# A four-layer graph network on one core: edge rows joined to sender rows in source order, and layer 1 computed beside its gather

## The chip, the cores and the metric

The kernel runs on 1 core of one Trainium2 chip. The metric is the device time of one execution in microseconds, median of three runs. Five engines work side by side, each with its own queue of instructions: PE (matmul), DVE (vector), ACT (scalar), POOL (GpSimd) and SP (which here only issues DMAs). They wait for one another and for DMAs by semaphores.

## The reference

3125 nodes with 64 features, 53125 directed edges `src -> dst` sorted by `dst`. Four layers, each `x = x + layer(relu(layernorm(x)))`:

```python
# layer 0: per source node, over its edges
feat = concat(seg_sum(edge_attr_32, src), seg_max(edge_attr_32, src), seg_mean(edge_attr_32, src), u)
out0 = relu(feat @ W1 + b1) @ W2 + b2
# layer 1: attention, 8 heads; loops are added to the edges
hx = h @ W; a_src, a_dst = per-head dot products of hx
logits = leaky_relu(a_src[src] + a_dst[dst], 0.2)
alpha = softmax of logits over the edges of each dst
out1 = mean over heads of segment_sum(hx[src] * alpha, dst) + bias
# layer 2: message = silu(concat(edge_attr_64, h[src], h[dst]) @ W1_msg + b1_msg)
out2 = upd(h, segment_mean(message @ W2_msg + b2_msg, dst))      # upd: two dense layers with silu
# layer 3: cosine similarity of Wh[src] and Wh[dst], weighted, summed over the edges of each src
```

`message @ W1_msg` splits into three parts: an edge part (`edge_attr_64` by the first 64 rows of `W1_msg`), a sender part and a receiver part.

## The kernel before, in words

The edges and one extra entry for each node, M = 56250, form a list of L = 128 x 440 entries. Two such orders exist: by source (`K.by_src`) and by destination (`K.by_dst`). Entry (p, j) is the place p*440 + j, so each of the 128 partitions holds 440 entries in a row. Sums over a node's edges are scans along the partition (`tensor_tensor_scan` with a mask that is 0 where a node begins), and a carry across partitions (`collect`). Work goes in NBLK = 10 blocks of TB = 44 columns. A column is fetched by one indirect DMA that POOL issues: 128 rows of a DRAM table, chosen by 128 indices. `gather_blocks` issues the 440 columns of a layer into a ring of two blocks (RING = 2); POOL waits until the block two before has been used.

The order of the work:

- `sort_sources`: a bitonic network on DVE (137 steps, 512 columns; short distances across partitions go through PE transposes and an ACT copy, `turn_blocks`, `keep_partners`) orders the list by source. In the same step `EdgeTable` multiplies `edge_attr_64`, given transposed as `edges_t`, by `W1_msg` on PE, ACT copies the result (line 610) and stores it as the table `recp`: an edge's row is the edge part and its source node (RE = 66 words).
- `layer0_pass`: POOL issues 440 gathers of `rec_s` rows (line 878; R0 = 36 words: `edge_attr_32`, two weights, the other node) in source order. DVE meanwhile sorts again (`sort_destinations`, here with two words for each entry, 1024 columns), `edge_order`, `list_setup` and `src_to_tiles` make index lists and masks, and `layer0_sums` scans block by block: ACT fills masks and turns rows (`fill`), DVE scans sums and maxima, ACT packs (`pack`), SP stores `sums0`.
- `layer0_finish`: POOL issues 22 edge gathers (`early_edges`, line 1351), 25 gathers of `sums0` at the last entry of each node (`collect`, line 1008), 60 more edge gathers; DVE and PE form the carries (line 1057 is the first use of the gathered sums), then two dense networks give the nodes and layer 1's table `tab1`.
- Layer 1: `layer1_gather` (line 831, 440 columns of R1 = 82 words) is stored as `g1` in tile order. When all of it is in, `layer1_softmax` works on 110 partitions x 512 entries (lines 1572 to 1625), `layer1_spread` makes the item weights, and `layer1_sums` runs 54 bodies of 12 items: DVE makes the weights (line 1847), PE multiplies (line 1831), DVE adds into `acc` (line 1855). Window, place and slot of each item are read into registers (line 1874). `layer1_tail` (from line 2029) divides by the sums, finishes x and stores the sender and receiver parts as table `tab2` of 2 x 3200 rows of R2 = 128 words. Beside all this POOL issues the remaining 358 edge gathers (lines 1379 and 1370) and eight stores of finished blocks to `rowsd` (line 1332).
- Layer 2: `layer2_gather` waits for `tab2` and the edge rows. POOL gathers 440 columns of `tab2` rows by the source node that came along in the edge row, word 64 of `u`. Each block: ACT turns the receiver half (line 2358), DVE scans it over the node's entries (line 2399), adds the edge part `u` (line 2407) and the sender half (line 2411), ACT applies silu, DVE scans, SP stores `sums2`. `layer2_tail` collects and makes layer 3's table.
- Layer 3: the same way in source order.

An engine's steps follow one another (`Step`); with `pool_ahead=True` POOL isn't held at the end of a step, so that its gathers run ahead of the other engines. `renew_semaphores` resets semaphores that counted far.

## Time and profile before

| | |
|---|---|
| runs | 3940.43, 3941.34, 3942.44 us, median 3941.34 |
| span of the profiled execution | 3095.7 us |
| the profiled execution's own time | not given; against the median of the runs 845.6 us lie outside the span |
| POOL busy | 2190.4 us (71%), 2299 instructions |
| DVE busy | 1326.6 us (43%) |
| PE busy | 610.1 us (20%) |
| ACT busy | 481.9 us (16%) |
| HBM | 154.17 MB read, 93.09 MB written, 80 GB/s over the span |

Busy time leaves out the issuing of DMAs on other engines, registers and semaphores. The span runs from the first to the last instruction of the program that the profiler recorded. Times in the timeline are counted from the span's start.

### The profile page before, as it was taken

How to read it: one execution, taken by the hardware profiler on the slowest of the kernel's cores; microseconds unless marked ns; L12 is line 12 of the kernel's file. 1: busy time of each engine (PE TensorE's matmuls, PEld its weight loads, DVE VectorE, ACT ScalarE, POOL GpSimd, SP SyncE). 2: the span in 40 equal slices, each digit the busy share in tenths (PEclk: the TensorE clock that was granted, in tenths of full speed). 3: DMA queues.
4: the chain of work that ended last, by engine and by line, in shares of the span. 5: the costliest groups of instructions: out<-in, count | busy, mean ns of one | idle time of the engine just before them, and what ended most of it. 6: DMA issues, size and time to landing. Idle time of an engine off the chain costs nothing.

```text
span 3095.7 us, 14532 instructions
## 1 busy us (share of the span) xinstructions
PE 610.1 (20%) x3300; PEld 466.1 (15%) x3301; DVE 1326.6 (43%) x1981; ACT 481.9 (16%) x447; POOL 2190.4 (71%) x2299
## 2 busy tenths in 40 slices
PE   5521130001410000001888860000000400000001
PEld 5411110001300000001676640000000300000001
DVE  8888885202310000008466643233244615353455
ACT  2200006211100000000000022223223212111220
POOL 0177777777777777777777777777777377777774
PEclk8665565555555555555899875555555555555555
DMA  9311114212344755645355424323232123223231
GB/s 325 112 25 14 14 27 100 64 34 63 66 52 53 67 57 60 65 52 65 106 135 155 111 50 74 109 91 128 91 109 92 45 56 85 78 72 91 72 90 52
DMA packets 192274, 248.04 MB, mean 80 GB/s; under 512 B 135507, under 2 KB 146381, under 8 KB 184662
## 3 DMA queue, kind: packets, MB, share of 16 engines
q0 software_dynamic: 74048, 114.24, 19.1%
q1 hardware_dynamic: 60102, 103.67, 10.0%
q10 hardware_dynamic: 58064, 29.51, 7.9%
q14 instruction: 45, 0.37, 0.0%
q8 instruction: 15, 0.25, 0.0%
HBM read 154.17 MB, written 93.09 MB: 80 GB/s over the span
## 4 chain that ended last, share of the span: by engine, by line
POOL 55%; issue 19%; DVE 2%; ACT 0%; DMA 0%; DVEq 0%; POOLq 0%; ACTq 0%
POOL l1g_rows L831 13%; POOL l2g_rows L831 13%; POOL l3g_rows L831 12%; POOL ep_rows L1370 11%; POOL ep_rows L1351 2%; POOL l2t_res L2457 1%; POOL l3t_res L2866 1%; POOL l0f_res L1008 1%; DVE l3g_banks L2813 0%; DVE l3g_banks L2837 0%; ACT l3g_banks L2771 0%; DVE l3g_banks L2834 0%; DVE l3g_dot L2820 0%; DVEq L2819 0%; POOL ep_rows L1379 0%
## 5 line engine op out<-in xcount | busy, mean ns | idle before, releaser
L878 POOL DMA_INDIRECT l0g_rows<-in_rec_s,ents x440 | 427.4, 971 | 137.6 <-issue 133.9
L831 POOL DMA_INDIRECT l2g_rows<-tab,ep_rows x440 | 416.8, 947 | 134.2 <-issue 134.2
L831 POOL DMA_INDIRECT l1g_rows<-tab,srct x440 | 416.8, 947 | 134.2 <-issue 134.2
L831 POOL DMA_INDIRECT l3g_rows<-tab,others x440 | 416.1, 946 | 134.2 <-issue 134.2
L1370 POOL DMA_INDIRECT ep_rows<-recp,entd x352 | 338.7, 962 | 107.3 <-issue 107.3
L1572 DVE TENSOR_TENSOR l1s_A<-l1s_bank,l1s_mk 110x512 f32<-110x512 f32 x8 | 5.2, 686 | 528.4 <-PE l1s_bank L1534 528.4
L1831 PE MATMUL l1a_pa<-l1a_g,l1a_wt 128*128 x1296 | 169.6, 291 | 0.0
L1831 PEld LDWEIGHTS l1a_pa<-l1a_g,l1a_wt 128*128 128x128 f32 x1296 | 158.9, 202 | 23.8 <-issue 23.8
L2811 DVE COPY l3g_banks<-l3g_q 128x65 f32<-128x65 f32 x12 | 2.7, 229 | 306.8 <-ACT l3g_banks L2771 306.4
L2397 DVE COPY l2g_mix<-l2g_q 128x64 f32<-128x64 f32 x11 | 2.5, 228 | 306.9 <-ACT l2g_mix L2358 306.9
L1534 PE MATMUL l1s_bank<-ident,atp 128*110 128x128 f32 x64 | 10.9, 347 | 539.7 <-ACT atp L1473 530.6
L2872 PE MATMUL l3t_nmp<-ident,l3t_nmb 128*64 128x128 f32 x2 | 0.7, 447 | 575.0 <-DVEq L2889 575.0
L1847 DVE TENSOR_TENSOR l1a_wt<-l1a_place,item_ex 128x1536 f32<-128x1536 f32 x54 | 94.9, 1757 | 7.7
L1351 POOL DMA_INDIRECT ep_rows<-recp,entd x82 | 79.1, 964 | 25.0 <-issue 24.7
L319 POOL IOTA iot<- 128x3200 f32 x1 | 2.8, 2803 | 130.0 <-DVE sorts_raw L335 130.0
L1473 ACT COPY atp<-l1g_rows 128x704 f32 (+1 forms) x10 | 8.3, 826 | 552.5 <-DMA l1g_rows<-tab,srct 552.5
L1534 PEld LDWEIGHTS l1s_bank<-ident,atp 128*110 128x110 f32 x64 | 10.4, 217 | 540.4 <-issue 531.1
L2771 ACT COPY l3g_banks<-l3g_rows 128x2860 f32<-128x2860 f32 (+3 forms) x12 | 55.2, 4599 | 220.8 <-DMA l3g_rows<-tab,others 220.7
L420 DVE TENSOR_TENSOR sortd_x<-sortd_x 128x512 f32<-128x512 f32 (+1 forms) x128 | 85.6, 669 | 4.2
L2872 PEld LDWEIGHTS l3t_nmp<-ident,l3t_nmb 128*64 128x64 f32 x2 | 0.3, 203 | 575.2 <-DVEq L2889 575.2
L421 DVE TENSOR_TENSOR sortd_x<-sortd_x 128x512 f32<-128x512 f32 (+1 forms) x128 | 84.5, 660 | 0.0
L2358 ACT COPY l2g_mix<-l2g_rows 128x2816 f32<-128x2816 f32 (+2 forms) x11 | 47.5, 4318 | 231.6 <-DMA l2g_rows<-tab,ep_rows 231.6
(582 smaller groups left out, 2330.2 us busy)
## 6 DMA issues: line engine op xcount, KB each, us to landing
l1a_g<-g SPq DMA_DIRECT2D x54, 390.0 KB
recp<-ep_rows ACTq DMA_DIRECT2D x11, 1320.0 KB, 5.9
g<-l1g_rows ACTq DMA_DIRECT2D x10, 1430.0 KB, 22.7
sums<-l0s_sums SPq DMA_DIRECT2D x10, 1408.0 KB, 5.1
sums<-l2o_sums SPq DMA_DIRECT2D x9, 1408.0 KB, 4.9
sums<-l3o_sums SPq DMA_DIRECT2D x9, 1408.0 KB, 5.3
rowsd<-ep_rows POOLq DMA_DIRECT2D x8, 1452.0 KB, 5.9
ep_rows<-rowsd SPq DMA_DIRECT2D x8, 1452.0 KB, 6.6
```

Source lines behind the costliest of these rows:

```text
L420: v.tensor_tensor(out[0], pair[0], pair[1], ALU.min).then_inc(step, 1)
L421: v.tensor_tensor(out[1], pair[0], pair[1], ALU.max).then_inc(step, 1)
L831: nc.gpsimd.indirect_dma_start(out=ring.rows[:, s, j, :], out_offset=None, in_=table, in_offset=bass.IndirectOffsetOnAxis(ap=index(b, s, j ...
L878: nc.gpsimd.indirect_dma_start(out=rows[:, j, :], out_offset=None, in_=K.a["rec_s"], in_offset=bass.IndirectOffsetOnAxis(ap=K.by_src.ent[: ...
L1008: nc.gpsimd.indirect_dma_start(out=res[:, w, :], out_offset=None, in_=table, in_offset=bass.IndirectOffsetOnAxis(ap=end[:, w:w + 1], axis= ...
L1351: nc.gpsimd.indirect_dma_start(out=ring.rows[:, s, j, :], out_offset=None, in_=K.recp, in_offset=bass.IndirectOffsetOnAxis(ap=K.by_dst.ent ...
L1370: nc.gpsimd.indirect_dma_start(out=ring.rows[:, s, j, :], out_offset=None, in_=K.recp, in_offset=bass.IndirectOffsetOnAxis(ap=K.by_dst.ent ...
L1831: nc.tensor.matmul(pa[b][:, bass.ds(places[u], P)], wt[:, b, u].rearrange("p h s -> p (h s)"), g[:, b, bass.ds(slots[u], P)], start=False, ...
L1847: v.tensor_tensor(wt[:, b], place[:, b].unsqueeze(2).to_broadcast([P, IB, H, WIN]), K.item_ex[:, :, bass.ds(n * IB, IB)].rearrange("p h i ...
L2358: nc.scalar.copy(cut(bank_of(i), n)[:, :, 1:], ring.rows[:, b % RING, c0:c0 + n, D:].rearrange("p j f -> p f j")).then_inc(spread, 1)
L2457: nc.gpsimd.indirect_dma_start(out=res[:, w, :], out_offset=None, in_=K.sums2, in_offset=bass.IndirectOffsetOnAxis(ap=by.end[:, w:w + 1], ...
L2771: nc.scalar.copy(cut(bank_of(i), C1, n)[:, :, 1:], ring.rows[:, b % RING, c0:c0 + n, C1:].rearrange("p j f -> p f j")).then_inc(spread, 1)
```

## The change

- `rec_s` rows grow to RR = 100 words, with `edge_attr_64` at their end; `edges_t`, `others`, `EdgeTable`, `recp` and `rowsd` go. Layer 0's gather fills a ring of two blocks, and POOL saves blocks 0 to 7 to `recd`; the sums load them back.
- `layer0_sums` also makes the edge part of layer 2 for blocks 0 to 8 (`EdgeRows`: ACT `move`, PE `project`, DVE `differ`), and a new `last_edges` that of block 9. It stores, in source order, the difference of each entry's edge part to the entry before it in the same run of one source, into `tabT`.
- `sort_destinations` sorts one word for each entry; `edge_order`, `early_edges` and `remaining_edges` go.
- Layer 1: `layer1_softmax`, `layer1_spread` and `layer1_sums` go. `layer1_items` and a new `layer1_marks` (masks of the nodes that cross a block's border) come ahead of a new `layer1_stream`, which does the softmax of each block as it lands, then 3 or 4 bodies (the last block 21), then 16 steps of a third sort (`OrderSort`), which gives for each entry in destination order its place in source order. Nodes that cross a border are joined in `layer1_borders`.
- `layer1_tail` writes the sender part, by 25 indirect DMAs, to the first entry of each source (`begin`) in `tabT`, and sender and receiver part to its end. A new step `source_rows` loads `tabT` block by block, scans it along each source's run and stores it back, so that each row becomes sender part plus edge part.
- `layer2_gather` gathers rows of 64 words of `tabT` by place (`by_dst.ent`); the receiver part is the row of a node's own entry, picked out by a DVE multiply in place of the ACT turn.

```diff
-R0 = 36
-RE = 66
+RR = 100
+SAVED = NBLK - 2
+QB = 11
+QH = H * QB
+SORT_STEPS = 137
+SORT_SHARE = 16
...
-            layer0_finish(K)
...
-                    layer1_gather(K)
-                    layer1_softmax(K)
-                remaining_edges(K)
...
-                        layer1_spread(K, T)
-                        layer1_sums(K)
-                    layer1_tail(K, T)
+            layer1_table(K)
...
+                    layer1_gather(K)
+                    layer1_items(K)
+                    layer1_marks(K, T)
+                    layer1_stream(K, T)
+                K.t2 = SourceTable(tail)
+                layer1_tail(K, T)
+            source_rows(K)
...
+def layer0_pass(K):
+                for b in range(NBLK):
+                    s = b % RING
+                    if b >= RING:
+                        pool.wait_ge(saved[s], b // RING * 16)
+                    for j in range(TB):
+                        if j == SETTLE and 1 <= b <= SAVED:
+                            pool.wait_ge(gathered[b - 1], TB * 16)
+                            nc.gpsimd.dma_start(K.recd[:, (b - 1) * TB:b * TB, :], ring[:, (b - 1) % RING]).then_inc(saved[(b - 1) % RING], 16)
+                        c = b * TB + j
+                        nc.gpsimd.indirect_dma_start(
+                            out=ring[:, s, j, :], out_offset=None, in_=K.a["rec_s"],
+                            in_offset=bass.IndirectOffsetOnAxis(ap=K.by_src.ent[:, c:c + 1], axis=0)
+                        ).then_inc(gathered[b], 16)
...
+UNIT_PAIRS = [(k, min(4, TB // 2 - k)) for k in range(0, TB // 2, 4)]
...
+    def project(self, pe, b):
+        for u, (k, n) in enumerate(UNIT_PAIRS):
+            i = b * NU + u
+            pe.wait_ge(self.packed, i + 1)
+            pe.wait_ge(self.moved, i) if i else None
+            for q in range(n):
+                lt = nc.tensor.transpose(self.turn[:, q * P:(q + 1) * P], self.at[:, 0, q * P:(q + 1) * P], self.K.ident[:, :])
+            lt.then_inc(self.flipped, 1)
+            pe.wait_ge(self.moved, i + 1)
+            pe.wait_ge(self.placed, i) if i else None
+            for q in range(n):
+                lt = nc.tensor.matmul(self.prod[:, q * P:(q + 1) * P], self.at[:, 1, q * P:(q + 1) * P], self.W[:, :],
+                                      start=True, stop=True)
+            lt.then_inc(self.multiplied, 1)
...
+    def differ(self, dve, b):
+        v.tensor_copy(E[:, 0, :], self.last[:, :])
+        for u, (k, n) in enumerate(UNIT_PAIRS):
+            i = b * NU + u
+            dve.wait_ge(self.multiplied, i + 1)
+            v.tensor_copy(E[:, 1 + 2 * k:1 + 2 * (k + n), :],
+                          self.prod[:, 0:n * P].rearrange("p (j d) -> p j d", d=D)).then_inc(self.placed, 1)
+        v.drain()
+            v.tensor_tensor(self.back[:, :, :], E[:, 0:TB, :], after.unsqueeze(2).to_broadcast([P, TB, D]), ALU.mult)
+        v.tensor_copy(self.last[:, :], E[:, TB, :])
+        v.tensor_tensor(E[:, 1:, :], E[:, 1:, :], self.back[:, :, :], ALU.subtract).then_inc(self.edged, 1)
...
+                for b in range(NBLK):
+                    pack(b)
+                    if b < NBLK - 1:
+                        edges.move(act, b)
+                    if b + RING < NBLK:
+                        fill(b + RING)
...
+def bodies_of(b):
+    ready = [min(TB * (i + 1) // IB, BODIES) for i in range(NBLK)]
+    ready[-1] = BODIES
+    return range(ready[b - 1] if b else 0, ready[b])
...
+                def weigh(n):
+                    tiles = values(nc, K.item_tile[0:1, n:n + 1, 0:IB].rearrange("p b i -> p (b i)"), mybir.EngineType.DVE, J - 1)
+                    for u in range(IB):
+                        i = n * IB + u
+                        lt = v.scalar_tensor_tensor(
+                            wt[:, n % 2, u], K.iot[:, 0:WIN].unsqueeze(1).to_broadcast([P, H, WIN]), S.item_rel[:, i:i + 1],
+                            S.ex[:, bass.ds(tiles[u], 1), :].rearrange("p a h -> p (a h)").unsqueeze(2).to_broadcast([P, H, WIN]),
+                            ALU.is_equal, ALU.mult)
+                    lt.then_inc(weighed, 1)
...
+                for b in range(NBLK):
+                    if b == NBLK - 1:
+                        order.entries(v, dve)
+                    soften(b)
+                    for n in bodies_of(b):
+                        if n >= 2:
+                            add(n - 2)
+                        weigh(n)
+                    order.advance(v, steps_of(b))
...
+                    pe.wait_ge(heaped, b + 1)
+                    for t in range(TB):
+                        lt = nc.tensor.matmul(sup[0:D + 1, b * 2 * H:(b + 1) * 2 * H], ring.rows[:, s, t, 0:D + 1], S.hw[:, t, :],
+                                              start=(t == 0), stop=(t == TB - 1))
...
+            @block.gpsimd
+            def _(pool):
+                for q, (w, n) in enumerate(quads):
+                    pool.wait_ge(tabled, q + 1)
+                    for k in range(w, w + n):
+                        nc.gpsimd.indirect_dma_start(out=K.tabT, out_offset=bass.IndirectOffsetOnAxis(ap=K.by_src.begin[:, k:k + 1], axis=0),
+                                                     in_=tab[:, k, 0:D], in_offset=None).then_inc(scattered, 16)
...
+def source_rows(K):
+                def load(b):
+                    if b >= 3:
+                        sp.wait_ge(S.stored[b % 3], b // 3 * 16)
+                    sp.dma_start(X[:, b % 3], rows[:, b * TB:(b + 1) * TB, :]).then_inc(loaded[b % 3], 16)
...
+                    nc.scalar.copy(mixes[b % 2][:, :, 1:], X[:, b % 3].rearrange("p j f -> p f j")).then_inc(spread, 1)
...
+                    nc.scalar.copy(X[:, b % 3], by_entry(mixes[b % 2][:, :, 1:])).then_inc(packed, 1)
...
+                    v.tensor_tensor_scan(flat(mix), flat(keeps[b % 2]), flat(mix), 0.0, ALU.mult, ALU.add)
...
-                gather_blocks(nc, pool, ring, K.tab2, lambda b, s, j: u[:, s, j, D:D + 1], ready, last)
+
+                gather_blocks(nc, pool, ring, K.tabT, lambda b, s, j: K.by_dst.ent[:, b * TB + j:b * TB + j + 1], ready, last)
...
+                    v.tensor_tensor(by_entry(mix[:, :, 1:]), ring.rows[:, s, c0:c0 + n, :],
+                                    begins[:, b * TB + c0:b * TB + c0 + n].unsqueeze(2).to_broadcast([P, n, D]), ALU.mult)
```

## Rows read from the trace of the kernel before

**Rows 1.** The page's head.

```profile
span 3095.7 us, 14532 instructions
```

**Rows 2.** The page's groups: line, engine, operation, out<-in, count | busy us, mean ns | idle before.

```profile
L831 POOL DMA_INDIRECT l2g_rows<-tab,ep_rows x440 | 416.8, 947 | 134.2 <-issue 134.2
```

**Rows 3.** POOL's timeline: start us, duration us, instruction, count, idle before.

```profile
140.34 1.10 POOL L878 DMA_INDIRECT l0g_rows<-in_rec_s,ents  x1 [3.71 <-ACTq L619]
...
729.47 0.95 POOL L1008 DMA_INDIRECT l0f_res<-sums,ends  x1 [0.31 <-issue]
...
841.60 0.98 POOL L831 DMA_INDIRECT l1g_rows<-tab,srct  x1 [0.30 <-issue]
...
1852.84 0.94 POOL L831 DMA_INDIRECT l2g_rows<-tab,ep_rows  x1 [0.30 <-issue]
```

**Rows 4.** Windows of the whole span.

```profile
core 0: us, PE busy (x) PEld busy (x) DVE busy (x) ACT busy (x) POOL busy (x), PEclk, DMA share, GB/s
...
840.00:1393.00 553.00, 11.77 (x24) 7.01 (x24) 13.64 (x43) 7.44 (x9) 417.84 (x442) 0.51 0.57 60
1393.00:1855.00 462.00, 325.13 (x2092) 253.46 (x2092) 292.40 (x353) 37.47 (x69) 351.91 (x369) 0.85 0.44 104
```

**Rows 5.** Groups by form, layer 2's gather.

```profile
L2399 DVE TENSOR_TENSOR_SCAN l2g_mix<-l2g_keeps,l2g_mix 128x2880 f32<-128x2880 f32 x9 | 55.5, 6161 | 0.7
...
L2358 ACT COPY l2g_mix<-l2g_rows 128x2816 f32<-128x2816 f32 x9 | 43.7, 4861 | 229.0 <-DMA l2g_rows<-tab,ep_rows 229.0
...
L2411 DVE TENSOR_TENSOR l2g_mix<-l2g_mix,l2g_rows 128x2816 f32<-128x2816 f32 x9 | 27.9, 3099 | 0.7
```

**Rows 6.** DVE's timeline.

```profile
195.98 0.70 DVE L420 TENSOR_TENSOR sortd_x<-sortd_x 128x512 f32<-128x512 f32 x1
...
407.40 0.69 DVE L533 TENSOR_SCALAR sortd_node<-sortd_x 128x1024 int32<-128x1024 int32 x1
...
492.18 3.15 DVE L972 TENSOR_TENSOR_SCAN l0s_totals<-l0s_keeps,l0s_feats 128x1440 f32<-128x1440 f32 x1
...
762.73 0.39 DVE L1057 TENSOR_TENSOR l0f_res<-l0f_res,colsums_bp 128x224 f32<-128x224 f32 x1 [28.85 <-DMA l0f_res<-sums,ends]
...
1769.72 0.34 DVE L2029 TENSOR_SCALAR l1f_rec<-acc 128x200 f32<-128x200 f32 x1 [0.38 <-PEq L223]
```

**Rows 7.** The page's groups, POOL at the first sort's end.

```profile
L319 POOL IOTA iot<- 128x3200 f32 x1 | 2.8, 2803 | 130.0 <-DVE sorts_raw L335 130.0
```

**Rows 8.** DMA issues: count, KB each, us to landing.

```profile
ep_rows<-rowsd SPq DMA_DIRECT2D x8, 1452.0 KB, 6.6
```

**Rows 9.** Groups by form, layer 0, the sort's turns and the column sums.

```profile
L610 ACT COPY ep_rows<-sorts_proj 128x512 f32<-128x512 f32 x55 | 31.9, 588 | 37.0 <-PE sorts_proj L595 31.4 <-DMA first_key<-keys 5.4
...
L488 PE MATMUL sortd_turn<-ident,sortd_x 128*128 128x128 f32 x112 | 27.6, 427 | 181.7 <-DVE sortd_x L448 149.1 <-DVE sortd_x L421 32.6
L943 ACT COPY l0s_sums<-l0s_totals 128x1408 f32<-128x1408 f32 x10 | 27.1, 2706 | 7.5 <-DMA sums<-l0s_sums 5.2 <-DVEq L980 2.3
...
L1020 PE MATMUL colsums_bp<-colsums_car,colsums_sel 128*128 128x65 f32 x50 | 10.9, 419 | 2.8 <-DVEq L1051 2.8
```

**Rows 10.** Groups by form, layer 1's softmax.

```profile
L1576 DVE TENSOR_TENSOR_SCAN l1s_A<-keepc,l1s_first,l1s_A 110x512 f32<-110x512 f32 x8 | 9.5, 1261 | 0.1
...
L1572 DVE TENSOR_TENSOR l1s_A<-l1s_bank,l1s_mk 110x512 f32<-110x512 f32 x8 | 5.2, 686 | 528.4 <-PE l1s_bank L1534 528.4
```

**Rows 11.** DVE's timeline, a carry of the softmax.

```profile
1454.59 0.37 DVE L1613 TENSOR_TENSOR_SCAN l1s_tot<-l1s_nmt,l1s_small 8x110 f32<-8x110 f32 x1 [0.47 <-PE l1s_small L1544]
```

**Rows 12.** One line's instructions, the register loads: ns min/median/max.

```profile
L1874 PEldq TENSOR_LOAD <-item_slot x54: 846/850/2959, 1512.8 to 1760.9; - x54
...
L1874 DVEq TENSOR_LOAD <-body_w x54: 300/305/1181, 1515.6 to 1765.6; - x54
```

**Rows 13.** PE's timeline, the passes of a body.

```profile
1574.38 2.94 PE L1831 MATMUL l1a_pa<-l1a_g,l1a_wt 128*128 x24
```

**Rows 14.** Windows of L878: stretch, us, POOL busy (x), PEclk, DMA share, GB/s.

```profile
200.00:400.00 200.00, 153.45 (x153) 0.50 0.13 14
```

More of the change, by code:

```diff
@@ L340, in _ @@
             def _(pe):
-                for i in range(AHEAD):
-                    edges.project(nc, pe, i)
                 pe.wait_ge(framed, 1)
@@ L1888 @@
 NS = len(SETS)
-TABS = 3
 def layer1_tail(K, T):
@@ L2249, in layer2_gather @@
         layer2_weights(K, T)
-        ring = Ring(ph, R2)
-        held, u = K.rows.ring.gathered, K.rows.ring.rows
+        ring = Ring(ph, D)
         mix_banks = ph.ps("mix", (P, 6 * 512))
@@ new lines, in last_edges, with _ @@
+def last_edges(K, edges):
+    nc = K.nc
+    with Phase(K, "er9") as ph:
+        edges.banks(ph)
+        with Step(nc, pool_ahead=True) as block:
+            @block.tensor
+            def _(pe):
+                edges.project(pe, NBLK - 1)
+            @block.scalar
+            def _(act):
+                edges.move(act, NBLK - 1)
+            @block.vector
+            def _(dve):
+                edges.differ(dve, NBLK - 1)
+            @block.sync
+            def _(sp):
+                edges.store(sp, NBLK - 1)
+                sp.wait_ge(edges.stored, NBLK * 16)
@@ new lines, with __init__ @@
+class SourceRows:
+    def __init__(self, K, ph):
+        self.ring = Ring(ph, R1)
+        self.kept = [ph.sem(f"kept{s}") for s in range(RING)]
+        self.stored = [ph.sem(f"stored{s}") for s in range(RING)]
+        self.got, self.headed, self.bordered = ph.sems("got", "headed", "bordered")
+        self.item_rel = ph.sb("item_rel", [P, ITEMS])
+        self.ex = ph.sb("ex", [P, J, H])
+        self.within = ph.sb("within", [P, J])
+        self.ends = ph.sb("ends", [P, 2, J])
+        self.hw = ph.sb("hw", [P, TB, 2 * H])
+        self.first = ph.sb("first", [P, R1])
+        self.heads = ph.sb("heads", [QH, NBLK])
+        self.border = ph.sb("border", [P, 2, NBLK])
+        self.window = ph.sb("window", [1, NBLK], I32)
```

1544 lines of the change are left out of this document (875 added, 669 removed).

## The prediction

> **What bounds the kernel now.** Read the page's head first: the span is 3095.7 us [rows 1], while the median run is 3941.3 us, so 845.6 us lie outside the span and no row says where. Below, the sum is made against the span and the 845.6 us are held constant; a rival drops that. Next the largest group: a gather of 128 rows costs POOL 0.947 us, and 134.2/440 = 0.30 us of issue stand before each, so 1.25 us [rows 2]. Three groups read like this one, and POOL issues 440 more gathers for edge rows: 82 early ones, then 358. Its timeline shows them back to back: layer 0 from 140.34, layer 1 from 841.60, layer 2 from 1852.84 [rows 3]. Then the windows: while layer 1 gathers, DVE is busy 13.6 of 553 us; in the next 462 us it is busy 292 us, and POOL gathers edge rows beside it [rows 4]. So POOL's queue sets the end nearly everywhere, and two stretches are open to change: 140 to 842 and 842 to 1853. The rest (layer 2's gather, its tail, layer 3) I leave as it is: layer 2's block trades an ACT turn of 4.86 us for a DVE multiply of 3.1 us beside a 6.16 us scan, two 3.1 us elementwise steps and small ones [rows 5], some 25 us for 55 us of POOL; its last part moves by 1 us at most.
>
> **Layer 0.** The gather: the row grows from 144 to 400 bytes; I hold the 1.25 us an issue, since layer 2's rows of 512 bytes cost as much [rows 2]. Eight saves of a block join POOL's queue, each between nothing and a gather's 1.25 us; I take 0.9: +7. A save waits for the previous block, ten gathers on, when that has long landed; reuse of a ring half waits for a save issued 34 gathers (42 us) before. Without the edge projection the start comes about 2 us earlier. End: 729.47 − 22 x 1.25 = 702.0 before [rows 3], 711 after with 2 to 5 us of slack for the landings.
>
> The DVE chain: the destination sort ran at double width from 196.0 to 407.4 [rows 6]. At single width it is the first sort, which held POOL's table back for 130.0 us [rows 7], some 126 us for the steps alone. It then ends at 321 or so. Of the 84.8 us from there to the first scan at 492.2 the edge order goes (a few shifts and one DMA of 6.6 us at most [rows 8]: 8 us); 77 us stay, plus a 2.25 MB reload that 6.6 us for 1452 KB scales to 10 us. The first scan is at about 407, 85 us earlier than before.
>
> But each block now carries the edge matmul inside the same chain. Per block: two scans of 3.15 [rows 6] with small steps 7.3; ACT's pack 2.71 for one half and about half of it for the other, 4.0, in front of the edge moves in ACT's order; first edge pack 0.6. Then six units, each one waiting for its own hand-offs: four transposes at 27.6/28 = 0.99, an ACT copy of 512 at 0.59, and four fp32 matmuls of N = 128. Fifty passes of N = 65 took 10.9 us, 0.22 each at the lower of the two clock levels [rows 9], so N = 128 costs 0.44, four 1.78. With 0.19 for hand-offs a unit is 3.55, five and a half of them 19.9 us. The copy of the last unit 0.6, multiply 3.1, difference 3.1, copy and drains 0.5. Sum 39.4 us a block. Nine blocks from 407 end at 762 to 766; so block 9 isn't scanned when its gather lands (713) but at 773, packed at 777, stored at 783. POOL's 25 gathers of sums wait for that store: 783 to 817, where they began at 729.47, behind 22 edge gathers that are gone. Behind it block 9's edge units and difference (28 us) run to 811 on DVE, before the column sums (7 of copies, 11 of PE): collect's first use comes at about 836 against 762.73 [rows 6]. So **+73 us**. Ends: units at the upper clock cost 6 us less a block, then 707 before block 9 and no lateness but that of the block itself, +20; dearer hand-offs (0.6 us in place of 0.2), +95.
>
> The node network behind it is unchanged, so layer 1's gather starts at 841.6 + 73 = 915. The 60 edge gathers before it (761 to 836) were under the DVE work and give nothing back.
>
> **Layer 1 to layer 2's gather.** Before: 1852.84 − 841.60 = 1011.2 us. Count from layer 1's first gather. The items and the marks (25 + 25 us), keys 8: block 0's softmax starts at +61, when block 0 (55 us) is in. Per block on DVE:
> - softmax on 88 partitions x 512: five scans (1.26 and 1.20) and five elementwise steps (0.69) 9.6 us [rows 10]; two carries across rows, each two trips to PE and back, of which one idle is 0.47 us [rows 11]: 3.8; exp and the turn back 2.0; twelve small multiplies and drains 4.1. 19.5 us.
> - 3.67 bodies (44 tiles, 12 to a body). A body: window load 0.31; two adds of 455 and 325 columns 1.07; a load of 12 registers, 0.85 us on PE [rows 12], 0.85 to 1.15 here; twelve multiplies of 128 columns, each 0.22 to 0.25 (0.39 for 224 [rows 6], 0.69 for 512). 5.4 us; 19.8 a block.
> - 16 steps of the third sort at 128.4/137 = 0.94: 15.5.
> - PE's 44 border matmuls before the bodies, 12 to 19 us, mostly beside the first weighings: 4.
> Sum 59 us (55 to 64) against POOL's 55.0. DVE falls behind by 4 a block; POOL, allowed two blocks ahead, then idles 12 us at most. Block 9 starts at +592, with entries of the sort 9.5, softmax 19.5: +621. In the last block 21 bodies are left (4 at the pace of the others, 17 that it takes up because there are 54), each 5.7: +741, the last adds +750. Borders 25: +775. Before, a body took 4.7 us from start to start; PE's 24 passes take 2.94 us [rows 13], so DVE sets it both times. The tail takes 79 of the 83 us between its first step at 1769.72 [rows 6] and layer 2's first gather; it stays, +855, with 6 us for scatters that land behind it.
>
> Then a new pass over the whole table: ten blocks are loaded, turned by ACT (2816 columns 4.86, both ways about 7.5 a block), scanned by DVE (6.16 for 2880 columns [rows 5], mask copy 1.7 to 3.1, small steps: 8.6 to 10) and stored, 2.88 MB a block by DMA. 1452 KB in 6.6 us gives 220 GB/s, 13 us, but that is one lone transfer with its latency of some 2 us; two are in flight here. I take 9.7 a block between 8.6 and 13, and 21 us of fill: +970. Landing, semaphores, layer 2's first gather: +977. POOL has nothing to issue in it. Result 977 − 1011 = **−34 us**. Ends: bodies at 4.8 or 6.8 shift it by −19 or +23; the streamed block at 55 or 64 by −36 or +45; the pass at 8.6 or 13 by −11 or +33.
>
> One row bears on DVE working beside POOL. In 200 to 400, beside the double-width sort, 153 gathers ran, 1.31 us each against 1.25 [rows 14], so 0.06 us a gather. If all of layer 1's 440 paid that, POOL's gather would take 575, not 551; in the sum DVE is behind anyway and only 10 us of it would show. The Trainium skill (GPSIMD Engine Reference, Key points) says of GpSimd: "Shares its SBUF interfaces with VectorE", with contention from DVE instructions with two SBUF inputs; by that rule each masked add, multiply and scan of the streamed layer slows the gather. The trace agrees in direction, with the 0.06 us above.
>
> **Sum.** 3095.7 + 73 − 34 = 3134.7 in the span; with 845.6 outside it 3980.3 us.
>
> **Rivals.**
> A, the forecast: between 3950 and 4020, 0.45. For it: the hand-off chain of layer 0 has no cover, since POOL waits for block 9's sums; the serial pass is pure addition.
> B, faster. The units run at the upper clock or overlap, and a streamed block fits into 55 us. It decides in layer 0 when a block takes under 34 us: +20 in place of +73. With a stream at 55 (−36 on −34) and the rest as in A this gives 3095.7 + 20 − 70 + 845.6 = 3891, with bodies at 4.8 and the pass at 8.6 3861, with layer 0 alone 3927; I put it at 3915. Against it: the clock is granted at 0.51 in layer 1's gather [rows 4]. 0.22.
> C, the terms cancel: within 0.2% (8 us, about what a measurement can tell from no change), 0.08.
> D, the time outside the span goes with POOL's DMAs. 2,278 indirect DMAs and 845.6 us make 0.37 us each. Then a gather really costs 1.62 us. Layer 1 to 2 took 1011 + 794 x 0.37 = 1306; now its gather takes 713 and DVE keeps up, so block 9's softmax ends at 744, bodies 120, adds 9, borders 25, tail and scatters 86, the pass and the start 116: 1100, −206. In layer 0 sums and edges hide behind a gather to 862, and the edge gathers behind it go: −12. About 3723. For it: nothing else of that size is in sight. Against it: no row inside the span shows one. 0.15. The Trainium skill (Runtime: NRT & Kernel Launch, The ~15µs preamble/postamble breakdown) puts the stages around a kernel at 9 to 15 us; by that rule the rest of the 845.6 us would have to belong to the execution. The times here show the 845.6 us and not their parts.
> E, dearer: a register load that DVE can't hide, hand-offs at 0.6 us, a streamed block at 64 us that stalls POOL, the pass at 13: 3941 + 95 − 34 + 20 to 100: 4020 to 4100. It decides when a body takes over 6.5 us. 0.10.
>
> **How the numbers follow.** Likeliest is A, so 3980. Its own range is 3950 to 4020. From 3860 to 4060 all of A and C, nearly all of B and half of E are held, 0.8; D lies below. Faster: B and D, 0.37. Same: C and the edge of A, 0.09. Slower: the rest, 0.54.
>
> **What would show it.** Right: layer 0's first scan near 407 and 39 us from scan to scan; POOL idle from 711 to 783; layer 1's first gather near 915 and its last one less than 565 later; 21 bodies 5.7 us apart at its end; a stretch of some 115 us between the tail and layer 2's first gather in which POOL has nothing. Wrong: a scan pitch under 34 or a body over 6.5 us; a span that changes by one amount and a run time by another (D); layer 2's block no longer under POOL's 55 us.

## The result and the profile after

The kernel after takes 4113.64 us (median of 4, 4108.22 to 4118.08) against 3941.36 (median of 4, 3940.43 to 3942.44) in the same job: 1.0437 times the time before, 95% interval 1.0422 to 1.0451. The forecast, 3980 in a range of 3860 to 4060, had the side right and the size wrong; the time lies 54 us above the range.

The page's head and groups, after (line, engine, operation, out<-in, count | busy us, mean ns | idle before it and what ended it):

```profile
span 4106.2 us, 18305 instructions
...
L699 POOL DMA_INDIRECT l1g_rows<-tab,srct x440 | 438.6, 997 | 493.6 <-PE l1s_sup L3009 361.9
L699 POOL DMA_INDIRECT l2g_rows<-tabT,entd x440 | 455.1, 1034 | 135.9 <-issue 135.9
...
L766 POOL DMA_INDIRECT l0f_res<-sums,ends x25 | 23.7, 946 | 445.9 <-DMA sums<-l0s_sums 438.6
```

The profiled execution of the kernel after took 4108.22 us, and 4106.2 of them are its span. Only 2.0 us lie outside, where [rows 1] with the median beside them left 845.6. So the kernel before, unchanged, was profiled again (`b0_before_again`): 3942.58 us, and its page and POOL's timeline read

```profile
span 3940.8 us, 14532 instructions
...
L878 POOL DMA_INDIRECT l0g_rows<-in_rec_s,ents x440 | 455.4, 1035 | 138.8 <-issue 135.0
...
L831 POOL DMA_INDIRECT l2g_rows<-tab,ep_rows x440 | 446.4, 1015 | 144.8 <-issue 144.8
```

```profile
141.82 1.10 POOL L878 DMA_INDIRECT l0g_rows<-in_rec_s,ents  x1 [3.73 <-ACTq L619]
...
955.32 0.94 POOL L1008 DMA_INDIRECT l0f_res<-sums,ends  x1 [179.79 <-DVEq L1027]
...
1123.76 0.98 POOL L831 DMA_INDIRECT l1g_rows<-tab,srct  x1 [0.31 <-issue]
...
2565.20 0.94 POOL L2283 DMA_INDIRECT l2g_first<-tab,node0nd  x1 [343.77 <-DMA tab<-l1f_tab]
```

The same instructions, but a gather of layer 2 takes 1.34 us with its issue ((446.4 + 144.8)/440) where [rows 2] give 1.25, the sums' gather starts at 955.32 and not at 729.47, layer 2's at 2565.20 and not at 1852.84 [rows 3]. (The instructions compared as a layer's first gather are not always the same one: 2565.20 is the gather of the nodes' own entries, 1.2 us ahead of the first column.) The execution whose profile stood ahead of the prediction was unlike all those whose span is on record; its own time is not. Every comparison below is with this second profile of before. POOL's timeline, after:

```profile
140.42 1.15 POOL L2363 DMA_INDIRECT l0g_rows<-in_rec_s,ents  x1 [3.05 <-DVE ents L337]
...
1176.90 0.94 POOL L766 DMA_INDIRECT l0f_res<-sums,ends  x1 [438.57 <-DMA sums<-l0s_sums]
...
1320.97 1.00 POOL L2637 DMA_INDIRECT l1g_first<-tab,node0c  x1 [113.11 <-SPq L1079]
...
2730.01 0.96 POOL L1660 DMA_INDIRECT l2g_first<-tabT,node0nd  x1 [112.62 <-DMA tabT<-t_X]
```

Up to layer 1's first gather after is 197.2 us later (1320.97 against 1123.76); from there to layer 2's first gather it is 32.4 us shorter (1409.0 against 1441.4); from layer 2's first gather to the end it is equal (1376.2 against 1375.6). 197.2 − 32.4 + 0.6 = 165.4, which is the difference of the spans.

What made the first profile another is read from DVE. The first two windows are 100 us of the second sort in before, in the early profile and in the later one. The third block is after: its first sort (20 to 120), in which POOL gathers nothing, its second sort (300 to 400), then two windows of layer 1, the first beside the gather (1470 to 1520), the second while POOL stands (1525 to 1560). Each row has the window and its length, then PE, PEld, DVE, ACT and POOL busy with counts, then granted clock, DMA share and GB/s:

```profile
300.00:400.00 100.00, 17.72 (x72) 14.12 (x72) 88.12 (x163) 6.70 (x18) 76.83 (x77) 0.50 0.13 14
```

```profile
300.00:400.00 100.00, 0.00 (x0) 0.00 (x0) 45.30 (x72) 0.00 (x0) 78.26 (x72) 0.50 0.11 13
```

```profile
20.00:120.00 100.00, 14.14 (x52) 8.59 (x52) 86.96 (x260) 6.48 (x25) 0.00 (x0) 1.00 0.00 0
300.00:400.00 100.00, 0.00 (x0) 0.00 (x0) 27.59 (x72) 0.00 (x0) 73.96 (x79) 0.50 0.30 84
...
1470.00:1520.00 50.00, 17.09 (x69) 14.04 (x69) 11.55 (x34) 0.00 (x0) 38.41 (x39) 0.50 0.24 48
1525.00:1560.00 35.00, 16.42 (x117) 14.74 (x117) 26.38 (x72) 2.09 (x3) 0.00 (x0) 0.50 0.54 37
```

Beside the gather DVE starts 72 instructions in 100 us, of 512 columns each in before and of 256 in after; without it 260. So it costs 1.39 us an instruction, whatever its width: that is why halving the sort's width gave nothing. In layer 1 it is the same: 34 instructions in 50 us beside the gather, 72 in 35 us without. In the early profile DVE starts 163 beside the same gather. DVE's timeline, after, shows where that goes: a first pause of 11 us some 28 us after the gather's start (9.3 us in before's later profile, none in its early one), and from then on two short instructions and 1.3 to 2.0 us of nothing:

```profile
179.16 1.53 DVE L626 TENSOR_TENSOR sets_inside<-sets_rows,sets_limit 128x1320 f32<-128x1320 f32 x1 [11.00 <-remote]
...
289.18 0.42 DVE L406 TENSOR_TENSOR sortd_x<-sortd_x 128x256 f32<-128x256 f32 x1 [1.34 <-DVE sortd_x L407]
289.52 0.42 DVE L407 TENSOR_TENSOR sortd_x<-sortd_x 128x256 f32<-128x256 f32 x1
291.97 0.43 DVE L406 TENSOR_TENSOR sortd_x<-sortd_x 128x256 f32<-128x256 f32 x1 [2.04 <-remote]
```

The second sort therefore ends at 743.5 in after and at 740.0 in before, both times just behind the gather's last column (738.3 and 732.3).

### The profile page after: what moved, and what is told of

Same layout as the page of the kernel before. It is cut to its first block and busy times, and to the rows that moved or that the text cites. A ratio compares the mean times of both kernels' runs of the same rounds, so it can differ in the third digit from the quotient of the medians.

```text
span 4106.2 us, 18305 instructions
## 1 busy us (share of the span) xinstructions
PE 931.5 (23%) x4290; PEld 730.0 (18%) x4290; DVE 1706.1 (42%) x3415; ACT 557.9 (14%) x552; POOL 1879.4 (46%) x1883
## 5 line engine op out<-in xcount | busy, mean ns | idle before, releaser
L699 POOL DMA_INDIRECT l1g_rows<-tab,srct x440 | 438.6, 997 | 493.6 <-PE l1s_sup L3009 361.9
L699 POOL DMA_INDIRECT l2g_rows<-tabT,entd x440 | 455.1, 1034 | 135.9 <-issue 135.9
L2983 PE MATMUL l1s_pa<-l1s_g,l1s_wt 128*128 x1296 | 299.5, 411 | 142.6 <-issue 142.3
L2983 PEld LDWEIGHTS l1s_pa<-l1s_g,l1s_wt 128*128 128x128 f32 x1296 | 287.8, 328 | 185.1 <-issue 185.0
L2937 DVE SCALAR_TENSOR_TENSOR l1s_wt<-iot,l1g_item_rel,l1g_ex 128x128 f32<-128x128 f32 x648 | 175.1, 347 | 59.3 <-issue 59.0
L406 DVE TENSOR_TENSOR sortd_x<-sortd_x 128x256 f32<-128x256 f32 (+1 forms) x128 | 53.7, 420 | 253.4 <-remote 208.9
L2948 DVE TENSOR_TENSOR l1t_acc<-l1t_acc,l1s_pa 128x455 f32 x108 | 55.6, 557 | 224.9 <-remote 111.4
L3009 PE MATMUL l1s_sup<-l1g_hw,l1g_rows 128*65 128x16 f32 x880 | 98.6, 269 | 28.4 <-DVEq L2931 28.4
L2474 DVE COPY er_E<-l0s_prod 128x512 f32<-128x512 f32 (+1 forms) x54 | 35.0, 647 | 164.9 <-PE l0s_prod L2437 164.9
L3009 PEld LDWEIGHTS l1s_sup<-l1g_hw,l1g_rows 128*65 128x65 f32 x880 | 97.6, 231 | 31.0 <-DVEq L2931 31.0
L2437 PE MATMUL l0s_prod<-er_W,er_at 128*128 128x128 f32 x396 | 83.8, 374 | 35.7 <-ACT er_at L2457 31.8
```

The lines of the kernel that those rows point to most:

```text
L406: v.tensor_tensor(out[0], pair[0], pair[1], ALU.min).then_inc(step, 1)
L699: nc.gpsimd.indirect_dma_start(out=ring.rows[:, s, j, :], out_offset=None, in_=table, in_offset=bass.IndirectOffsetOnAxis(ap=index(b, s, j ...
L2437: lt = nc.tensor.matmul(self.prod[:, q * P:(q + 1) * P], self.at[:, 1, q * P:(q + 1) * P], self.W[:, :], start=True, stop=True)
L2474: v.tensor_copy(E[:, 1 + 2 * k:1 + 2 * (k + n), :], self.prod[:, 0:n * P].rearrange("p (j d) -> p j d", d=D)).then_inc(self.placed, 1)
L2937: lt = v.scalar_tensor_tensor(wt[:, n % 2, u], K.iot[:, 0:WIN].unsqueeze(1).to_broadcast([P, H, WIN]), S.item_rel[:, i:i + 1], S.ex[:, bas ...
L2948: lt = v.tensor_tensor(sums, sums, sums_of(pa[n % 2], lo, hi), ALU.add)
```

## The experiments

The theory: POOL's indirect gathers hold DVE (and what waits for it) to about one short instruction a gather, so that work laid beside a gather is hardly hidden, and each removed gather frees more than its own time. The rivals: the slow pace is that of the sort's own semaphore waits; or of the volume and the landings of the DMAs; or the time is simply the added work and has nothing to do with the gather.

**Both kernels again.** 

> The kernel before, unchanged. The profile shown of it has a span of 3095.7 us beside a median of 3941.4 us, the changed kernel's profiled run took 4108.2 us with a span of 4106.2. Theory M (semaphore traffic): an execution of either kernel can run with semaphore updates held up while POOL issues gathers, and the timed runs of before did so while the one shown in the profile did not; then this profile has a span near 3940 us, and DVE's sort beside the gather waits about 2 us in places. Theory O (something outside the span): the span is near 3096 us again and 845 us lie outside it.

 Measured 3942.58 us, span 3940.8.

> The changed kernel, unchanged, on the same chip. Theory M: a span near 4108 us again, with the second sort spread over some 450 us. Theory O, and any theory in which the changed kernel's profile is the odd one: a span near 3200 us.

 Measured 4125.55 us, span 4123.5. Outside the spans lie 1.8 and 2.0 us: the 845.6 us are inside, in both kernels.

**Is it the semaphore waits?** In both kernels the sort's steps wait with a drain in place of the semaphore that DVE itself has raised:

```diff
-                dve.wait_ge(step, steps)
+                v.drain()
```

> The changed kernel; inside its three sorts DVE no longer waits for its own semaphore between two steps, but drains. Waits for PE and ACT stay. Theory M (semaphore updates arrive late while POOL gathers): the second sort, 468 us beside the gather, falls to 220 to 280, the third sort's share of a block from up to 60 us to 20 to 30, and the time by 200 to 350 us. Theory P (DVE's instructions themselves run slower beside the gather): the second sort stays above 440 us and the time within 20 us.

 Measured 4132.45 us (4123.88 to 4139.88), 1.0469 times before (1.0450 to 1.0488).

> The kernel before with the same edit in its two sorts. Theory M: its double-width sort, 472 us beside the gather in an ordinary execution, falls to 300 to 360, and the time by 80 to 180 us, less than in the changed kernel. Theory P: no change.

 Measured 3952.41 us, 1.0020 times before (1.0010 to 1.0030). In 300 to 400 DVE still starts 73 (after) and 72 (before) instructions. The next kernel goes further: it raises the sort's semaphore in the last step of a pass alone, so that hardly an instruction signals.

> The changed kernel; in its three sorts DVE drains between steps, as in the run with drains, and a step adds to the semaphore only where PE reads its result (28 of 274 halves), so that nearly all increments are gone. In the run with drains a drain behind one increment took 1.33 us beside the gather and behind two 2.70. Theory U (each semaphore update that an engine sends takes about 1.35 us while POOL gathers): the second sort falls from 468 to 200 to 260 us, the third sort's share from up to 60 to about 20 us a block, the time by 150 to 350 us. Theory K (what is slow beside the gather is the drain, or the step itself): no change, within 20 us.

 Measured 4123.77 us, 1.0447 (1.0429 to 1.0464). The drain's durations, ns min/median/max, then first and last start, with the gather (first row) and in the first sort without it (second):

```profile
L452 DVEq DRAIN  x35: 1329/2696/3396, 293.7 to 398.0; - x35
...
L452 DVEq DRAIN  x88: 300/731/733, 20.0 to 119.3; - x88
```

With waits, drains, signals or hardly any, the pace is the same: the waits are not the cause.

**Is the gather the cause?** POOL holds layer 0's gather until the second sort is done:

```diff
+                v.drain().then_inc(K.hold, 1)
...
+                pool.wait_ge(K.hold, 1)
```

> The changed kernel; POOL holds layer 0's gather until the second sort is done, nothing else. Theory M: the sort takes 130 us as the first one did, the gather runs from about 320 to 900, and what follows it is earlier than in the changed kernel, where the sort ended at 744 and the sums at 1170: the time falls by 100 to 250 us though the gather starts 180 us later. Theory S (layer 0's loss is only the edge arithmetic on DVE's chain, 35 us a block): the time rises, since the gather is delayed by 180 us.

 Measured 4128.97 us, span 4127.0. The window of 200 to 300 in the second sort, and the gather's start:

```profile
200.00:300.00 100.00, 13.38 (x48) 7.87 (x48) 87.52 (x261) 6.23 (x24) 0.00 (x0) 0.50 0.00 0
```

```profile
323.06 1.11 POOL L2366 DMA_INDIRECT l0g_rows<-in_rec_s,ents  x1 [185.70 <-DVEq L2315]
...
1331.98 1.01 POOL L2640 DMA_INDIRECT l1g_first<-tab,node0c  x1 [117.75 <-SPq L1079]
```

The sort takes 129 us by itself (193 to 322) and 467 beside the gather (276 to 743): the gather is the cause. Yet nothing is won, where a fall of 100 to 250 us was expected. The gather now runs from 323 to 921, and the sums' blocks, which can begin at 490, lie beside it. DVE's timeline, the first scan of blocks 0 to 4:

```profile
490.52 3.15 DVE L2574 TENSOR_TENSOR_SCAN l0s_totals<-l0s_keeps,l0s_feats 128x1440 f32<-128x1440 f32 x1
...
667.91 3.15 DVE L2574 TENSOR_TENSOR_SCAN l0s_totals<-l0s_keeps,l0s_feats 128x1440 f32<-128x1440 f32 x1
...
852.75 3.15 DVE L2574 TENSOR_TENSOR_SCAN l0s_totals<-l0s_keeps,l0s_feats 128x1440 f32<-128x1440 f32 x1
...
955.19 3.15 DVE L2574 TENSOR_TENSOR_SCAN l0s_totals<-l0s_keeps,l0s_feats 128x1440 f32<-128x1440 f32 x1
...
989.12 3.15 DVE L2574 TENSOR_TENSOR_SCAN l0s_totals<-l0s_keeps,l0s_feats 128x1440 f32<-128x1440 f32 x1
```

Beside the gather a block takes 177 and 185 us, behind it 34, though the last columns of block 1 are issued at 433, long before its scan at 668. The tenth scan starts at 1166.8, 6 us later than in after (1160.4). The gather holds up whichever chain of short steps lies beside it.

**Which part of a gather?** Layer 0's columns come by 440 direct DMAs on POOL, of the same shape but of consecutive rows, not the indexed ones (so layer 0 sums other rows):

```diff
-                        nc.gpsimd.indirect_dma_start(
-                            out=ring[:, s, j, :], out_offset=None, in_=K.a["rec_s"],
-                            in_offset=bass.IndirectOffsetOnAxis(ap=K.by_src.ent[:, c:c + 1], axis=0)
-                        ).then_inc(gathered[b], 16)
+                        nc.gpsimd.dma_start(ring[:, s, j, :], K.a["rec_s"][c * P:(c + 1) * P, :]).then_inc(gathered[b], 16)
```

> The changed kernel; in layer 0 POOL fetches each column by a direct DMA of 128 rows in place of an indirect one (the wrong rows). Issues take 0.9 us, not 1.25. If the slow pace hangs on the indirect kind, DVE's second sort beside them takes 130 to 200 us. If it hangs on POOL's DMAs of 128 rows as such, the sort is as slow as long as they last (about 400 us).

 Measured 3695.09 us. The group, and 50 us in which it runs beside the sort:

```profile
L2363 POOL DMA_DIRECT2D l0g_rows<-in_rec_s x440 | 232.8, 538 | 2.7 <-DVE ents L337 2.7
```

```profile
210.00:260.00 50.00, 5.58 (x20) 3.33 (x20) 44.38 (x130) 2.65 (x10) 50.00 (x96) 0.50 0.63 186
```

130 instructions in 50 us, the pace of a DVE alone, although the DMAs move 186 GB/s, more than twice the 84 of after, and POOL issues more of them. So it is the indirect kind and not the volume or the landings. The second sort lasts 129 us (195 to 324), and layer 1's first gather starts at 904.4, 417 us earlier. What of the 417 is the pace and what POOL's shorter issue (0.54 us a DMA against 1.35), this run doesn't part.

Next, 32 rows a gather in place of 128 (the other rows are zeros):

```diff
-                            out=ring[:, s, j, :], out_offset=None, in_=K.a["rec_s"],
-                            in_offset=bass.IndirectOffsetOnAxis(ap=K.by_src.ent[:, c:c + 1], axis=0)
+                            out=ring[0:32, s, j, :], out_offset=None, in_=K.a["rec_s"],
+                            in_offset=bass.IndirectOffsetOnAxis(ap=K.by_src.ent[0:32, c:c + 1], axis=0)
```

> The changed kernel; each of layer 0's 440 gathers fetches 32 rows, not 128 (the others stay zero). If the slow pace hangs on the number of DMAs, the second sort still takes about 468 us. If it hangs on the rows (descriptors), DVE gets far more than 72 instructions in 100 us, and the sort ends well before the gather.

 Measured 4122.85 us. DVE starts 73 instructions in 300 to 400, POOL 73 gathers (72 and 79 in after), and the second sort takes 467 us again. A quarter of the rows doesn't make DVE faster: the price goes by the DMA and not by its rows.

**What do the 440 edge gathers of before cost?** Before without the early and the remaining ones; layer 2 takes its indices from the source list and adds a piece of the node's own row in place of the edge part:

```diff
-                remaining_edges(K)
...
-            for c in range(first, first + n):
+            for c in range(first, first):
```

> The kernel before without its 440 gathers of edge rows, their eight stores and eight reloads; layer 2 takes its indices from layer 1's list and adds the receiver half where the edge part was, so the arithmetic is of the same size. It measures what the removed gathers cost. Sum by the profile shown of before: layer 0 -27, softmax to sums about -5 (DVE's work ended 2 us before POOL's): about -35 us. Theory M: the network after layer 0 (121 us), softmax (222) and spread (305) run beside these gathers and fall to 65, 77 and 45: the time falls by 450 to 550 us.

 Measured 3466.72 us against 3945.15 for before in that job; the spans are 3464.9 and 3940.8, 476 us apart. Layer 1's first gather starts at 1039.0 (−85), and from there to layer 2's it takes 1051.1 us in place of 1441.4 (−390): the softmax, spread and bodies ran beside those gathers. So the change removed something worth 476 us, and what it put in its place costs 282 us up to layer 1's gather (1321.0 against 1039.0) and 358 us behind it (1409.0 against 1051.1). 282 + 358 − 476 = 164 of the 165.4 us; this sum closes by construction, and what it says is only where the new work costs.

**Layer 0's edge part alone.** The edge arithmetic of blocks 0 to 9 on PE, ACT and DVE is left out and zeros are stored in `tabT`:

```diff
     def project(self, pe, b):
-        nc = self.K.nc
...
+        pass
...
+        if b == 0:
+            v.memset(self.E[:, :, :], 0.0)
+        v.drain().then_inc(self.edged, 1)
```

> The changed kernel without the arithmetic of the edge part in layer 0: ACT's packs, PE's transposes and matmuls, DVE's copies, product and difference are left out, and zeros are stored. In the forecast this arithmetic costs 30 us a block and hides beside the gather except at its end (+73 us in all). If the sort beside the gather ends at 744 in any case, nothing is hidden: the time falls by 230 to 300 us.

 Measured 3898.0 us, 216 less than after's median (230 to 300 was expected); layer 1's first gather starts at 1103.7 in place of 1321.0. Of the 282 us, 217 are the edge part in the sums; the saves, loads and stores of the wide rows are still in this kernel and share the other 65 with whatever else differs.

**The third sort alone.** Its steps are not made, and layer 2 gathers in the unsorted order:

```diff
-        for i in range(n):
-            self.cur = next(self.steps)
+        self.cur = self.X[0]
```

> The changed kernel without the steps of its third sort; layer 2 then gathers in a wrong order. If the sort costs its clean length, the time falls by 130 us or less. Theory U: its steps beside the gather take 3 to 4 us, not 0.94, and the stream of layer 1 gets shorter by 200 to 350 us.

 Measured 4050.89 us, 63 less than after's median, 75 less than its second profiled run. The stream runs from 1381 to 2442 in place of 1385 to 2500: 54 us, 5 to 6 a block, where the sum had 15.5. So more than half of the third sort did lie beside other things, and it is not what made the stream long; the 200 to 350 us of the second expectation did not come.

**The third sort in one piece.** All 137 steps stand in block 0's share. POOL, two blocks ahead, is then held, and most of them run without a gather:

```diff
-SORT_SHARE = 16
+SORT_SHARE = 137
```

> The changed kernel with all 137 steps of the third sort behind block 0's bodies, not 16 to a block. POOL then has one block to gather and stops, so most steps run with no gather beside them. Theory U: about 170 us for the sort in one piece against 13 to 60 us in each of nine blocks: the time falls by 60 to 200 us. If a step costs the same anywhere, the time stays or rises by up to 55 us, since POOL idles.

 Measured 4157.4 us, 1.0539 (1.0521 to 1.0556): 44 us slower than after. The first expectation, a gain of 60 to 200 us, is missed; the rise lies within the second, in which a step costs the same anywhere and POOL idles. POOL's longest wait is now 127.8 us (54.5 in after), its eight waits 424.1 us (361.9). The sort in one piece takes 145 us (1476 to 1621), and the first two softmaxes are 186 us apart in place of 97; the later blocks win about 5 us each (95.5 in place of 100.8), and that is less than the piece costs.

**Is overlap in layer 1 worth anything?** POOL's gather of a block waits until DVE is through with the block before, so the two never overlap:

```diff
+                if b:
+                    pool.wait_ge(S.serial, b)
...
+                    v.drain().then_inc(S.serial, 1)
```

> The changed kernel; in layer 1 POOL starts the gather of a block only when DVE has finished all work on the block before, so that nothing lies beside a gather. If the streamed work were hidden as in the forecast, each of nine blocks would lose up to 40 us of overlap: +300 us or more. Theory R (beside a gather DVE and PE get about 72 instructions in 100 us, so short instructions gain next to nothing there): within 60 us of the changed kernel.

 Measured 4254.5 us, +141. Waits on POOL (what waited, for whom: us, times, longest), in this kernel and then in after:

```profile
POOL l1g_rows L699 <- DVEq L2966: 615.3, 9, 81.3
```

```profile
POOL l1g_rows L699 <- PE l1s_sup L3009: 361.9, 8, 54.5
```

The same step of the softmax, once a block, in the serial kernel (ns min/median/max, first and last start):

```profile
L2921 DVE TENSOR_TENSOR l1s_F<-l1s_A,l1s_F x10: 686/687/689, 1409.8 to 2496.9; 88x512 f32<-88x512 f32 x10
```

A serial block takes (2496.9 − 1409.8)/9 = 120.8 us, one in after 100.3 (its row stands below), so overlap is worth 20.5 us a block. The whole stream is only 155 us longer (1270 against 1115), because block 0's softmax starts 31 us sooner after the layer's first gather once POOL stands. The +141 lies between the two expectations, under 60 and over 300 us. Full overlap would be worth the shorter of the two, POOL's gather of 55 us a block; it is worth 37% of that.

**What follows for the kernel.** If the price is paid by short instructions beside gathers and by serial chains, the edge part should go where no gather runs: under the first sort, where before had it. This kernel keeps the rest of the change (one joined row, single-width second sort, streamed layer 1, `source_rows`). PE multiplies `edges_t` beside the first sort and the joined row of 100 words goes to a table in DRAM; the sums of layer 0 only take the difference:

```diff
+                    edges.project(nc, pe, i)
...
-                            out=ring[:, s, j, :], out_offset=None, in_=K.a["rec_s"],
+                            out=ring[:, s, j, :], out_offset=None, in_=K.recj,
...
-                    edges.project(pe, b)
```

> The changed kernel with the edge matmul back under the first sort, as before the change: PE and ACT write edge part and the other 36 words as one row of 100 words, layer 0 gathers that row, and of the edge arithmetic only the difference (two long DVE instructions a block) is left in the sums. If the loss of layer 0 is the place of the matmul, with no gather beside it and 3.6 us a unit, layer 1's gather starts some 230 us earlier than in the changed kernel (at about 1090, 1326 there) and the time is 3860 to 3910, below both kernels. If the joined row or its saves are what costs, the time stays above 4000.

 Measured 3914.72 us (3910.95 to 3917.94), 0.9929 times before (0.9912 to 0.9945). It beats both kernels: 27 us (0.7%) under before in the same job, 199 under after. The time is 5 us above the range that was expected, and layer 1's first gather comes 192 us earlier than in after, not 230. A block of the sums is now two scans and two elementwise steps of the difference; DVE's timeline, one block:

```profile
855.33 3.15 DVE L2607 TENSOR_TENSOR_SCAN l0s_totals<-l0s_keeps,l0s_feats 128x1440 f32<-128x1440 f32 x1
...
858.92 3.16 DVE L2612 TENSOR_TENSOR_SCAN l0s_feats<-l0s_bounds,l0s_feats 128x1440 f32<-128x1440 f32 x1
...
862.46 3.03 DVE L2522 TENSOR_TENSOR er_back<-er_work,afters 128x2752 f32<-128x2752 f32 x1
...
868.09 3.09 DVE L2531 TENSOR_TENSOR er_E<-er_work,er_back 128x2816 f32<-128x2816 f32 x1 [2.20 <-DMA tabT<-er_E]
```

Its ten blocks are 16.9 us apart, layer 1's first gather starts at 1129.1 (+5 against before), where 1090 was expected, and from there to layer 2's first gather it takes 1412.3 (−29).

## Why the prediction missed

**The step that failed** is the first: "845.6 us lie outside the span"; "the 845.6 us are held constant". They are inside an ordinary execution: 282 up to layer 1's first gather (1123.8 against the 841.6 of [rows 3]), 430 from there to layer 2's (1441.4 against 1011.2), 133 behind it (1375.6 against 1242.9). Of the last, some 80 are the 880 gathers themselves at 1.34 us for 1.25. Of the 430, 390 are what the edge gathers hold back (the kernel without them takes 1051.1), and the 282 hold the second sort's slow pace, 467 us where the early profile has 212. What the change moves is just such work. Of what the forecast lacks between the spans (+165.4 measured, +39 forecast), 124 us lie ahead of layer 1's first gather and 2 behind it; so in the sum the term that failed is layer 0's +73, and in it the work that was to lie beside the gather. The side came out right by that chain, whose price a block was right. Two products in the sum are slightly off, 5.5 units of 3.55 us (19.5, not 19.9) and 16 steps of 0.94 us (15.0, not 15.5); neither matters. Point by point:

- *Second sort, −85 us.* "It then ends at 321 or so", "the first scan is at about 407". Measured: the sort's end 743.5, 3.5 later than in before, the first scan 834.6 in place of 856.4. So −22, and none of it is the width: it lies between sort and sums, where the edge order went. The forecast's 126 us for the steps hold where no gather runs (129 in the held kernel).
- *Layer 0's block, 39.4 us.* Near: 36.2, where before had 9.0 (856.4 to 937.1). The first scans of ten blocks start (1160.4 − 834.6)/9 apart. The unit's period, forecast 3.55, is 3.60, and PE's product is what DVE waits for:

```profile
1002.04 0.69 DVE L2474 COPY er_E<-l0s_prod 128x512 f32<-128x512 f32 x1 [2.92 <-PE l0s_prod L2437]
1005.64 0.69 DVE L2474 COPY er_E<-l0s_prod 128x512 f32<-128x512 f32 x1 [2.92 <-PE l0s_prod L2437]
```

  What was missed is how much of it shows: since the sort ends with the gather, no block lies beside it, and (36.2 − 9.0) x 9 = 245 us are added, less the 22. The gather of the sums is 221.6 later (forecast +54). The 60 edge gathers of before, which "were under the DVE work and give nothing back", gave back 24 of it (144.1 from the sums' gather to layer 1's, 168.4 in before): 197.2 against +73.
- *A streamed block, 59 us, "POOL then idles 12 us at most".* Measured 100.3, from a row of the softmax (ns min/median/max, first and last start): (2350.9 − 1447.9)/9. POOL idles 361.9 in eight waits. That is 57 us of POOL's gather and 43 in which POOL stands and DVE does what it couldn't beside it. The serial kernel above parts the miss of 41 us: there POOL waits 615.3/9 = 68.4 us a block for DVE, so 9 us are work that the sum of 59 priced too low, and the other 32 are overlap that didn't come. The forecast had the shorter side whole beside the longer one; 20.5 us of it are.

```profile
L2919 DVE TENSOR_TENSOR l1s_F<-l1s_A,l1s_F x10: 686/687/689, 1447.9 to 2350.9; 88x512 f32<-88x512 f32 x10
```

- *Layer 1 to layer 2's gather, −34 us.* Measured −32.4, and that is chance: 977 was forecast and 1409.0 measured, 1011.2 was read and 1441.4 is ordinary. Both sides of the difference were short by 430 and 432. Where there is no gather beside the work, the terms hold: bodies of the last block 6.3 us (forecast 5.7), borders 22 (25), tail 79.2 (79), the pass over the table 107.3 from 2614.1 to 2721.4 (97 and its fill), POOL's idle in it 112.6 (some 115). The bodies on DVE's timeline:

```profile
2450.46 3.24 DVE L2937 SCALAR_TENSOR_TENSOR l1s_wt<-iot,l1g_item_rel,l1g_ex 128x128 f32<-128x128 f32 x12 [1.07 <-issue]
2454.69 1.03 DVE L2948 TENSOR_TENSOR l1t_acc<-l1t_acc,l1s_pa 128x455 f32 x2 [0.99 <-PE l1s_pa L2986]
2456.78 1.40 DVE L2937 SCALAR_TENSOR_TENSOR l1s_wt<-iot,l1g_item_rel,l1g_ex 128x128 f32<-128x128 f32 x5 [1.06 <-issue]
```

- *Layer 2's block, "under POOL's 55 us".* Right: 1376.2 against 1375.6.
- *The rivals.* B's sign, a scan pitch under 34 us, didn't come (36.2). D came nearest in kind: the time outside does go with POOL's indirect DMAs. But it laid 0.37 us on each of them as POOL's own, where a gather costs 1.25 to 1.35 us and not 1.62, and so it freed DVE where DVE is held, and came out at −218. What D lacked is a price on the other engine: at 1.39 us an instruction the second sort alone moves the first scan from 407 to 835. E named no cause that came: a body took 6.3 us, under its 6.5, and the hand-offs were those of A. The Trainium skill (Runtime: NRT & Kernel Launch, The ~15µs preamble/postamble breakdown) leaves 9 to 15 us for the stages around a kernel; the runs leave 1.7 to 3.0 us between span and time, less than that, and agree with what follows from it, that the rest belonged to the execution.

Two things stay open. One is why the first profiled execution of before ran without the slow pace, with the same instructions and the same gathers: none of those profiled since did. So the gather is needed for the slow pace, but it isn't the whole condition. The other is what in an indirect DMA holds DVE. The pause and the slow pace set in some 28 us after the gather's start, and neither comes beside direct DMAs; no run was made to tell why.

## What to carry to other kernels

Compare the profile's span with the time before the first row is believed: if hundreds of microseconds are missing, as here, profile the kernel again; here the profile was of another kind of execution, and the missing time was not a constant. Do not call short vector work "hidden" beside an indirect gather on POOL; measure how many instructions the other engines start in 100 us with the gather and without it, and lay serial chains of short steps (sorts, hand-offs between PE, ACT and DVE) where no gather runs, long scans beside it. A removed gather is worth what it held back on other engines, here 476 us, and what replaces it must be priced in the place where it goes.

## What the runs showed of the hardware

Beside POOL's indirect DMAs (one in 1.23 to 1.39 us) DVE starts 71 to 73 instructions in the window from 300 to 400 in all twelve kernels that have them there, whether they are of 256 or 512 columns, wait on semaphores, drain, or hardly signal, and whether a gather brings 128 rows or 32. The one exception is the early profile of before, with 163. DVE starts 260 without a gather, and 130 in 50 us beside direct DMAs of 0.54 us each that move 186 GB/s. Work of few and long instructions pays little: layers 2 and 3, with scans of 3 to 6 us beside their gathers, have some 30 DVE instructions in 100 us (292 from 2800 to 3800 in after) and stay at POOL's pace. The other way round the effect is small: layer 1's gather costs POOL 1.25 us in the serial kernel, where DVE works on no block beside it, and 1.30 in after. The Trainium skill (GPSIMD Engine Reference, Key points) names contention between the two engines at their shared SBUF interfaces, with DVE instructions that have two SBUF inputs or run in a 2-port perf mode. The sort's instructions have two such inputs and run at full pace beside 440 direct DMAs of POOL, so the page's rule by itself doesn't account for what was measured here.
